# Both batches of a delta-rule scan in step: the order of six matmuls on TensorE and four operations on VectorE

## The reference

```
def step(S, inp):
    qi, ki, ui, wi = inp
    attn = jnp.tril(qi @ ki.transpose(0, 1, 3, 2))
    u_i = ui - wi @ S
    o_i = qi @ S + attn @ u_i
    return (S + ki.transpose(0, 1, 3, 2) @ u_i, o_i)
S0 = jnp.zeros((b, h, dk, dv), dtype=q.dtype)
S, o = jax.lax.scan(step, S0, (mov(q), mov(k), mov(u), mov(w)))
```

## Time and profile before

| | us |
|---|---|
| median of 3 runs | 594.73 |
| lowest and highest of them | 591.89, 598.05 |
| the profiled execution | 600.54 |
| its span, first to last instruction | 598.8 |
| PE, DVE, ACT, POOL busy in it | 439.1, 322.3, 225.3, 142.4 |
| mean granted TensorE clock | 0.821 |

### The profile page before, as it was taken

How to read it: one execution, slowest core, us unless ns; L and a number is a source line. 1 busy time by engine, 2 the same in 40 slices (tenths; PEclk the granted TensorE clock), 3 DMA queues, 4 the chain that set the end, 5 groups by cost and what they waited for, 6 DMA issues and landing times. The chain is left out here.

```text
span 598.8 us, 12845 instructions
## 1 busy us (share of the span) xinstructions
PE 439.1 (73%) x5009; PEld 333.1 (56%) x5010; DVE 322.3 (54%) x819; ACT 225.3 (38%) x453; POOL 142.4 (24%) x154
## 2 busy tenths in 40 slices
PE   0782699926976588899999999995999344029990
PEld 0682399913545467677875655563355344029890
DVE  4540355436965697776444654327368884216533
ACT  1232045514565278884231000017457222005550
POOL 4336025520006980000000000002023200733441
PEclk9999889966897679999679965558799655559996
DMA  9963301130000000000000000005400036140015
GB/s 174 261 199 88 101 15 37 35 89 1 0 1 0 4 4 4 5 4 3 1 2 1 2 0 1 0 1 123 106 1 1 0 120 197 44 128 24 32 35 155
DMA packets 32710, 29.93 MB, mean 50 GB/s; under 512 B 6800, under 2 KB 25776, under 8 KB 32656
## 3 DMA queue, kind: packets, MB, share of 16 engines
q1 hardware_dynamic: 23760, 20.96, 12.6%
q10 hardware_dynamic: 6400, 3.08, 3.4%
q0 software_dynamic: 2496, 5.13, 2.6%
HBM read 16.54 MB, written 9.21 MB: 43 GB/s over the span
## 5 line engine op out<-in xcount | busy, mean ns | idle before, releaser
L303 ACT ACTIVATE hT<-bank,b1s 128x128 f32<-128x128 f32 x184 | 52.4, 370 | 90.8 <-PE bank L260 90.6
L206 POOL DMA_INDIRECT ysort<-Y,row x46 | 44.8, 974 | 78.7 <-DVE Y L382 72.6
L260 PE MATMUL bank<-xT,w1s 128*128 (+1 forms) x368 | 51.5, 285 | 2.8 <-DVE xT L405 2.8
L276 PE MATMUL bank<-W,hT 128*128 x368 | 50.8, 281 | 3.6 <-ACT hT L303 3.1
L260 PEld LDWEIGHTS bank<-xT,w1s 128*128 128x128 f32 x368 | 47.0, 200 | 4.1 <-DVE xT L405 3.6
L1386 POOL TENSOR_TENSOR m_DSQ<-DEL 128x512 f32<-128x512 f32 x4 | 4.1, 1041 | 187.8 <-POOLq L767 185.1
L276 PEld LDWEIGHTS bank<-W,hT 128*128 128x128 f32 x368 | 45.2, 193 | 6.0 <-issue 5.8
L1056 DVE TENSOR_TENSOR d_BD<-bank,quarter 128x2048 f32<-128x2048 f32 x16 | 36.6, 2289 | 14.2 <-PE bank L760 14.2
L199 POOL DMA_INDIRECT xsort<-xr,pos x32 | 31.4, 981 | 48.4 <-DVE pos L361 39.3
L901 PE MATMUL bank<-XN,K 32*128 32x128 f32 x128 | 40.2, 403 | 1.6 <-DVE XN L1092 1.6
L966 ACT ACTIVATE d_BD<-d_TP 32x512 f32<-32x512 f32 x64 | 40.6, 634 | 0.9
(11 more groups left out here) (297 smaller groups left out, 939.4 us busy)
## 6 DMA issues: line engine op xcount, KB each, us to landing
W<-in_L_ffn_w SPq DMA_DIRECT2D x2, 2048.0 KB, 13.4
xsort<-pad ACTq DMA_DIRECT2D x2, 1483.5 KB, 23.1
xs<-xsort SPq DMA_DIRECT2D x10, 258.0 KB, 4.3
G<-ysort SPq DMA_DIRECT2D x8, 256.0 KB, 3.8
b2bc<-in_L_ffn_b SPq DMA_DIRECT2D x2, 512.0 KB, 20.3
m_pairs<-FS SPq DMA_DIRECT2D x4, 256.0 KB, 5.0
m_pairs<-firT SPq DMA_DIRECT2D x4, 256.0 KB, 4.9
m_pairs<-VP SPq DMA_DIRECT2D x4, 256.0 KB, 5.1
```

What stands on the lines that cost most here:

```text
L206: gp.indirect_dma_start(ysort, bass.IndirectOffsetOnAxis(row[:, t:t + 1], 0), Y[:, t, :], None).then_inc(y_stored, 16)
L260: mm = pe.matmul(pH[s % 2][:, j * P:(j + 1) * P], w1s[:, s, j * P:(j + 1) * P], xT[:, bass.ds(t, 1), :], start=True, stop=True)
L276: mm = pe.matmul(pY[s % 2][:, 0:D], hT[:, s % 2, j, :], W2[:, bass.ds(e, 1), j, :], start=(j == 0), stop=(j == FC - 1))
L303: act.activation(hT[:, s % 2, j, :], pH[s % 2][:, j * P:(j + 1) * P], ACT.Gelu, bias=b1s[:, s, j:j + 1]).then_inc(h_ready, 1)
```

## The change

On PE each step issues w for both batches, q for both, then a for both; on DVE both subtracts, then both states. The matmuls and operations, their operands and their waits stay the same; the number of instructions too. `turn_fl` and `v_stats` stay at the end of a step. Batch 1 no longer runs half a step behind, and nothing of it is left after the loop.

```diff
                 for n in range(STEPS_S):
                     w_state(0, n)
-                    if n > 0:
-                        add_state(1, n - 1)
+                    w_state(1, n)
                     if n == STEPS_S // 2:
 
                         pe.wait_ge(fl_taken, NG)
                     q_state(0, n)
+                    q_state(1, n)
                     add_state(0, n)
-                    w_state(1, n)
-                    q_state(1, n)
+                    add_state(1, n)
                     if 2 * n < NT:
                         turn_fl(2 * n)
                         turn_fl(2 * n + 1)
-                add_state(1, STEPS_S - 1)
...
                 for n in range(STEPS_S):
                     subtract(0, n)
-                    if n > 0:
-                        state(1, n - 1)
+                    subtract(1, n)
                     state(0, n)
-                    subtract(1, n)
+                    state(1, n)
                     if n % 8 == 7:
                         if n == 7:
                             ve.wait_ge(vsq_ready, 1)
                         v_stats(n // 8)
-                state(1, STEPS_S - 1)
```

## The result

The changed kernel takes 569.34 us (median of 4, 564.4 to 578.9) against 594.82 (591.89 to 598.05): a ratio of 0.954, 95% interval 0.946 to 0.963. The forecast was 589.9, range 580.5 to 599.5. It missed: the gain is 25.5 us, not 4.8.

What follows compares the result with a forecast made beforehand. The prediction took the order on PE, neither chain nor engine alone, to bound the full-clock scan steps. Its terms, -3.0 + 0 - 1.75 = -4.8 us, took the median 594.73 to 589.9 us, range 580.5 to 599.5.

Steps and rivals of the forecast that it cites:

- The 17 steps up to the last compared w0: Full-clock scan up to w0 of step 17: 34.94 us instead of 37.94, a term of -3.0 us.
- Plain steps: Scan steps without transposes at full clock: 1.90 us against 1.95 in the old order.
- the delay by the reductions of step 15: Reductions hold up both next subtracts, so a0 goes 0.8 us later, after step 7 as after step 15.
- The half-clock step: Plain scan step at half clock: 3.03 us as before, term 0, with -0.5 to +0.5 for 14 steps.
- The end: From w0 of step 31 to `intra`: 3.55 us instead of 5.30, a term of -1.75 us.
- The reductions after step 23: In the half-clock part of the scan, they hold a0 by less, about as they do now: 0.
- the forecast as reckoned: Main case for the whole kernel, -4.8 us in sum, 589.9 us from the median; chance 0.53.
- the clock falls later: Rival: in the scan, the clock falls after step 23 or not at all, -9.0 or more on top, 581 or below; chance 0.19.
- Two a's don't follow at once: Rival: a to a on PE takes 0.42 at full clock and 0.72 at half; total +2.7, 597.4; chance 0.05.
- Loads of the same rows are exposed: Rival: weight loads in scan steps show, some 22 us less the 4.8, 612; chance 0.02.
- The clock falls earlier: Rival: in the scan, the clock falls after step 7, +9.0, total +4.2, 598.9; chance 0.13.
- The change does nothing: Rival: both batches' chains stay bound by DVE and PE as before, only the tail shortens, 593; chance 0.08.

Runs made afterwards that it cites:

- the kernel with longer gaps: New order, with two pairs of reductions after step 7 and two after step 15, none later, against the changed kernel's spacing: 594.95 us, ratio 1.019.
- the control: Kernel before, old order, pairs of reductions after steps 7 and 15 kept, the other two pairs moved after the last state: 589.01 us, ratio 1.004.

## Why the prediction was wrong

**The order's own worth: right, a little small.** The 17 steps up to the last compared w0 were forecast at 34.94 us and took 333.34 - 299.56 = 33.78. Plain steps were 1.86 to 1.87 for 1.90, those with transposes 2.00 for 2.03, a1 came 0.23 behind a0 for 0.22, the delay by the reductions of step 15 0.6 for 0.8. The half-clock step was forecast at 3.03 and is 3.02 in the kernel with longer gaps. The end was forecast at 3.55 at half clock and takes 362.19 - 360.01 = 2.18 at full. The reductions after step 23, put at nothing, delay the a's by 0.6 at full clock.

**The clock: the step that failed.** I kept the fall of the old profile where it was, "the forecast as reckoned", with 14 steps at 3.03. Both profiles of the changed kernel have 1.00. Fourteen steps at 1.86 instead are 14 x 1.17 = 16.4 us, and the end 1.4: with them the sum would have been -22.6, and the measured change of scan is -22.8. (The 1.2 us less in the first 17 steps and the 0.6 more after step 23, both left out of this, partly cancel.) The rival *the clock falls later* named this mechanism, but I gave it 0.19 and priced it at one period of eight steps, "-9.0 or more", so that the range ended at 580.5, on its price, and left out the case of no fall.

**Why I weighed it wrongly.** I had seen that the fall came within 2 us of PE's longest wait, and reckoned the new wait as just as long, 0.8 us against 0.78. It is 0.52. Two sizes were off. The 0.8 was the delay of a0, not the time that PE stands: by my own terms q1, started at 0.72, runs 0.38 to 1.10, and a0 at 1.83 leaves 0.73. And the delay was too long: I let the reductions start at 0.18 in the step and subtract 0 at 1.49, and they start at 330.97 - 330.89 = 0.08 and subtract 0 at 332.16 - 330.89 = 1.27, so that a0 goes at 1.58, and q1 ends at 1.06. Then I took one wait of that length as what decides. With 1.12 or more PE lost the clock in the profiles of the new order; it kept it with 0.98 after step 7 in one, and with 0.52; in the old order 0.78 lost it, and with DVE's order alone four waits of 0.37 or less did. So the runs show that PE's standing makes the clock fall, and that the changed kernel in most executions stands too little for that. They give no length as the limit. The rows of before could not have settled it either: no fall at all was a case to be priced to the end of the scan, at about -23, beside the one that I kept.

**Rivals.** *Two a's don't follow at once* falls by the 0.23. *Loads of the same rows are exposed* falls: q's weights load from 329.38, when the w's on the same 128 rows run until 329.65, and the two w's and two q's follow one another at about 0.23 (timeline after). The rule of the Trainium skill (TensorE: Matmul & The Clock Gate, Part 3, What overlaps and what doesn't) that a weight load overlaps with a running matmul only on other row groups doesn't hold for this case. *The clock falls earlier* came in the new order only with longer gaps, after step 7 with the pairs. *The change does nothing* falls by the order's own worth above.

## What to carry to other kernels

Where a stretch of many small, dependent matmuls runs, look in the profile for the place at which the granted clock fell and at what PE waited for just ahead of it: here 1.3 us of reductions on another engine cost 15 us in the steps behind them. Price a change once with the clock kept and once without, each to the end of the stretch. Cut side work on the engine in the chain into pieces that fit its waits. Fit both engines' orders to one another: here VectorE's new order alone was 7% slower than before, and TensorE's alone 13%.

## What the runs showed that I had not expected

- The half clock, once there, stayed to the scan's end although PE was nearly always busy by the profile (47.93 of 48.57 us in the control). It came back within `intra`: in the control the mean is 0.62 over the 3.4 us behind the scan.
- Useless work on PE paid: 16 transposes, 16.7 us.
- In the profiles the clock outlived one wait of 0.98 us in the new order, and didn't outlive a row of waits of 0.37 or less with DVE's order alone.
- The same reductions, by placement alone: in the old order 568.9 (after the scan), 574.4 (one by one), 589.5 to 594.8 (in pairs); in the new one 562.7, 563.2 (spread), 569.3 and 566.3 (in pairs), 595.6 (in threes), 595.0 (in fours).
